# Splitting the feed-forward down products into three rounded products

## The reference, cut to what matters

```python
h = jnp.square(jax.nn.relu(jnp.einsum('bsd,fd->bsf', x, W_fc)))   # 256 -> 1024
y = jnp.einsum('bsf,df->bsd', h, W_proj)                          # 1024 -> 256
def step(mem, _):                                                 # five times
    reset = spike_fn(mem - THRESHOLD)
    mem_new = BETA * mem + y - reset * THRESHOLD
    return (mem_new, spike_fn(mem_new - THRESHOLD))
x = x + jnp.tanh(g_ffn[0]) * jnp.sum(spks, axis=0) / NUM_STEPS    # x: layernorm before W_fc
```

## Time and profile before

| | us |
|---|---|
| median of 3 runs (961.02 to 965.24) | 961.07 |
| profiled execution, its own time | 971.35 |
| its span | 969.6 |
| TensorE busy in it | 865.0 (89%) |
| VectorE, Pool, ScalarE busy | 546.8, 320.6, 306.4 |
| first up product to last down product of the feed-forward | 445.54 to 554.93 |

### The profile page before, as it was taken

One profiled execution on the slowest core, in us unless ns is written; L12 is line 12 of the kernel. 1 busy time (PEld: TensorE's weight loads), 2 busy tenths in 40 slices (PEclk: granted clock), 3 DMA queues, 4 the chain that ended last, 5 costly groups with the idle time before them and its releaser, 6 DMA issues.

```text
span 969.6 us, 12914 instructions
## 1 busy us (share of the span) xinstructions
PE 865.0 (89%) x4206; PEld 638.3 (66%) x4207; DVE 546.8 (56%) x1090; ACT 306.4 (32%) x656; POOL 320.6 (33%) x337
## 2 busy tenths in 40 slices
PE   6886699999785899987999979999999689999995
PEld 5454455554454555545888757777777579999994
DVE  4957646562476556642544378889888623333331
ACT  3555133233262333334333223222222012222230
POOL 4255244234146533441000114444443222232221
PEclk9999578899696889996999989999999879999999
DMA  9370000000000000008200082000000155555520
GB/s 302 117 308 27 1 0 1 1 1 1 0 1 0 1 1 0 1 1 288 55 0 0 1 283 75 11 12 11 12 11 12 54 192 198 201 167 168 200 81 4
DMA packets 32134, 67.87 MB, mean 70 GB/s; under 512 B 3161, under 2 KB 23095, under 8 KB 30999
## 3 DMA queue, kind: packets, MB, share of 16 engines
q1 hardware_dynamic: 28887, 56.63, 17.0%
q0 software_dynamic: 2624, 10.49, 3.4%
q10 hardware_dynamic: 578, 0.18, 0.1%
HBM read 55.20 MB, written 13.01 MB: 70 GB/s over the span
## 4 chain that ended last, share of the span: by engine, by line
PE 73%; DVE 15%; ACT 5%; issue 3%; DMA 2%; POOL 1%; DVEq 0%; SPq 0%; ACTq 0%; POOLq 0%
PE PS L1772 8%; PE PS L1760 8%; PE PS L639 7%; PE PS L1163 6%; PE PS L1145 6%; PE PS L1012 6%; PE PS L1000 5%; PE PS L630 4%; PE PS L610 4%; DVE NM L709 3%; PE PS L631 3%; PE PS L663 2%; PE PS L575 2%; PE PS L1147 2%; PE PS L649 2%
## 5 line engine op out<-in xcount | busy, mean ns | idle before, releaser
L817 ACT ACTIVATE EX<-PS 128x512 f32<-128x512 f32 x144 | 79.3, 594 | 173.2 <-PE PS L631 170.7
L709 DVE TENSOR_REDUCE NM<-PS 128x1 fp32r<-128x1101 f32 x64 | 82.7, 1302 | 73.9 <-PE PS L610 73.8
L800 POOL TENSOR_TENSOR sumP<-sumP,EX 128x1024 f32<-128x1024 f32 x32 | 75.8, 2368 | 42.2 <-ACT EX L817 41.2
L1760 PEld LDWEIGHTS PS<-xeT,w 128*128 128x128 f32 x736 | 85.7, 192 | 3.9 <-DMA w<-in_L_ffn_W 1.6
L1760 PE MATMUL PS<-xeT,w 128*128 128x128 f32 x736 | 86.1, 276 | 2.3 <-DMA w<-in_L_ffn_W 1.4
L1772 PE MATMUL PS<-w,heT 128*128 x368 | 83.3, 380 | 1.7 <-DVE oe L1702 1.7
L639 PE MATMUL PS<-EX,V 128*64 128x512 f32 (+1 forms) x288 | 75.3, 641 | 0.0
L1772 PEld LDWEIGHTS PS<-w,heT 128*128 128x128 f32 x368 | 68.3, 191 | 10.3 <-issue 2.1
L1163 PE MATMUL PS<-vw,pcT 128*128 128x256 f32 (+1 forms) x320 | 73.1, 384 | 1.2 <-ACT pcT L1355 1.2
L630 PE MATMUL PS<-QA,KA 100*128 100x512 f32 x144 | 70.3, 488 | 1.2 <-ACT EX L817 1.2
L1163 PEld LDWEIGHTS PS<-vw,pcT 128*128 128x128 f32 (+1 forms) x320 | 59.7, 191 | 8.8 <-issue 1.3
(11 more groups left out here) (260 smaller groups left out, 1586.9 us busy)
## 6 DMA issues: line engine op xcount, KB each, us to landing
w<-in_L_ffn_W SPq DMA_DIRECT2D x31, 1024.0 KB, 5.4
vw_rows<-vwn SPq DMA_DIRECT2D x2, 1232.0 KB
kwH_rows<-kwH SPq DMA_DIRECT2D x1, 2464.0 KB
kwL_rows<-kwL SPq DMA_DIRECT2D x1, 2464.0 KB
kwH<-kwH_rows POOLq DMA_DIRECT2D x1, 2464.0 KB, 12.5
kwL<-kwL_rows POOLq DMA_DIRECT2D x1, 2464.0 KB, 17.7
vw<-vw_rows SPq DMA_DIRECT2D x2, 1152.0 KB, 15.1
XR<-in_x SPq DMA_DIRECT2D x4, 512.0 KB, 14.2
```

Of the source, the lines that this page charges most:

```text
L709: dve.tensor_reduce(NM[:, n % 2, t // GT, SHIFT + t % GT:SHIFT + t % GT + 1], PSf[:, 512 * at:512 * at + KEYS], AX.X, ALU.max, negate=True ...
L800: pool.tensor_tensor(sumP[:], before, EX[:, (KT * n + c) % EB, :, :], ALU.add).then_inc(pool_summed, 1)
L817: act.activation(EX[0:r, k % EB, i, :], PS[0:r, ST_AT + i, :], ACT.Exp).then_inc(exp_done, 1)
L1760: last = pe.matmul(PS[:, 1 + 2 * p + c // 4, c % 4 * P:c % 4 * P + P], w1[:, u, k, c * P:c * P + P], xeT[:, p, k, :], start=k == 0, stop=k ...
```

## The change

The down products become three rounded products, as the up products are already. The inner values `h` get a high part `hH` (ScalarE's square, rounded on writing) and a rest `hL`: Pool computes the square once more in full format into one of two `square` tiles, and VectorE subtracts `hH` from it. The down weights get two parts in `wp`, made by Pool during the attention; the split of the up weights moves ahead of the first batch's attention, since `wp` takes the place of the unsplit up weights `wfc`. Two semaphores are new: `squared` (Pool's square is done) and `h_low` (VectorE's subtraction is done).

```diff
     def pe_ffn ... group
             pe.wait_ge(h_ready, FC * g + FC)
+            pe.wait_ge(h_low, FC * g + FC)
...
                     for c in range(FC):
-                        last = pe.matmul(PS[:, 4 + half, s * D:s * D + D], hT[:, c, at:at + P], wprojT[:, c, :],
-                                         start=c == 0, stop=c == FC - 1)
+                        for h, a in ((hH, 0), (hH, 1), (hL, 0)):
+                            last = pe.matmul(PS[:, 4 + half, s * D:s * D + D], h[:, c, at:at + P], wp[:, c, a, :],
+                                             start=c == 0 and h is hH and a == 0, stop=c == FC - 1 and h is hL)
...
     def act_ffn ... group
                 act.wait_ge(h_done, FC * g + c + 1)
+                if c >= 2:
+                    act.wait_ge(squared, FC * g + c - 1)
                 act.activation(relu[:, c % 2, :], PS[:, 2 + c % 2, :], ACT.Relu).then_inc(relu_ready, 1)
...
-                act.activation(hT[:, c, :], relu[:, c % 2, :], ACT.Square).then_inc(h_ready, 1)
+                act.activation(hH[:, c, :], relu[:, c % 2, :], ACT.Square).then_inc(h_ready, 1)
...
+    def pool_ffn(pool):
+        def group(g, last_group):
+            for c in range(FC):
+                pool.wait_ge(relu_ready, FC * g + c + 1)
+                if c >= 2:
+                    pool.wait_ge(h_low, FC * g + c - 1)
+                pool.tensor_tensor(square[:, c % 2, :], relu[:, c % 2, :], relu[:, c % 2, :], ALU.mult).then_inc(squared, 1)
+                if c == 1 and not last_group:
+                    pool_root(pool, g + 1)
...
     def dve_ffn
+        def low_parts(g, cs):
+            for c in cs:
+                dve.wait_ge(squared, FC * g + c + 1)
+                dve.wait_ge(h_ready, FC * g + c + 1)
+                dve.tensor_tensor(hL[:, c, :], square[:, c % 2, :], hH[:, c, :].bitcast(F32), ALU.subtract).then_inc(h_low, 1)
         z_low(0)
         with dve.Fori(0, NG - 1) as g:
             dve.wait_ge(g_zT, g + 1)
-            ffn_norm(dve, g + 1)
+            ffn_stats(dve, g + 1)
+            low_parts(g, range(4))
+            ffn_z(dve, g + 1)
+            low_parts(g, range(4, FC))
             z_low(g + 1)
             spike(g)
+        low_parts(NG - 1, range(FC))
...
+    def pool_wproj(pool):
+        pool.wait_ge(wfc_split, 2)
+        pool.tensor_copy(wp[:, :, 0, :], wprojT[:]).then_inc(wfc_split, 1)
+        pool.wait_ge(wfc_split, 3)
+        pool.tensor_tensor(wp[:, :, 1, :], wprojT[:], wp[:, :, 0, :].bitcast(F32), ALU.subtract).then_inc(wfc_split, 1)
...
         pool_project(pool, 0)
+        pool_wfc(pool)
         pool_attend(pool, 0)
         pool_project(pool, 1)
-        pool_wfc(pool)
+        pool_wproj(pool)
         pool_attend(pool, 1)
```

## The result

The changed kernel took 983.78 us (median of four runs, 979.2 to 988.66), the kernel before 963.15 beside it (961.02 to 965.24): a ratio of 1.0215, 95% interval 1.0143 to 1.0287. Slower, as forecast (983.7). The close agreement is luck: the four runs lie in two pairs, near 979.5 and 988.3, with the median between them, and the terms of the sum come to +17.4 us in the stage that the change touches, not to the +22.6 forecast. The same kernel run again (e0) gave 1.0142 [1.0098, 1.0186].

A forecast was written before the change was run, and what follows sets the result against it. TensorE's products were taken to bound the feed-forward stage. Terms 15.0 + 4.9 + 4.0 - 6.6 + 5.3 = +22.6 raised the profiled 971.35 to 994; less the profiled run's 10.3 above the median, 983.7 us, range 967 to 997.

The forecast's parts named there:

- waits, groups 1 to 4: Before each group's down products, the new square and subtraction chain adds 4.9, 7.5, 7.5 and 4.0 us.
- products: Down products on TensorE: 96 rounded products per group replace 64 records, 1.65 us less per group, -6.6 in all.
- clock: Down stages: TensorE's idle gaps make the granted clock fall in three of four, 1.75 us each, +5.3; bounds 0 and 7.
- Rival 1: Squares and subtractions run side by side without exclusion; only late root and longer chain count: +4.2, 965 us; chance 9%.
- I take 1.2: Pool's square of 512 columns takes 1.2 us, from a line through 462 and 1024 columns; bounds 0.60 and 1.3.
- I take 1.25: VectorE's four normalisations between the square and subtraction pairs cost 1.25 us, chosen between no cost and 1.38.
- The root's end: Pool's root in the middle groups ends at 483.6, 1.55 us after the statistics; squares three to eight wait behind it.
- two subtractions, 1.2: Last group: after the spike step ends at 533.5, two subtractions take 1.2 us before the third square begins at 534.7.
- the early release: Pool and VectorE exclude each other but for the last 0.15 us, so a square holds about 1.06, a subtraction 0.54.
- Linear between them: Down product of 256 columns takes 0.1295 us, between rows of 208 columns (0.110) and 512 columns (0.2335).
- Rival 3: Down products reach 0.110 us each, gaining 14.1 in all and outweighing the waits: 958 us, faster; chance 5%.
- Its other condition: The faster-products rival decides only if the waits before the down products stay under 14.1 us.

The follow-up runs named there:

- e0: The changed kernel run again with nothing altered: 979.91 us, ratio 1.0142 to the kernel before.
- e4: Changed kernel without Pool's squares and VectorE's subtractions, the third product taking the high part again: 953.24 us, ratio 0.9880 to the kernel before.
- e1: Changed kernel with VectorE's subtraction taking its first operand from an unused PSUM bank, square left out of the rest: 968.77 us, ratio 1.0044 to the kernel before.
- e3: Changed kernel with the next group's statistics and root taken one group earlier, full result computed: 975.52 us, ratio 1.0117 to the kernel before.
- e9: Changed kernel with both the subtraction reading PSUM (square left out) and the root one group earlier: 965.16 us, ratio 1.0014 to the kernel before.
- e5: Changed kernel with squares, subtractions and waits kept, but one full-format down product per chunk, rests left out: 992.34 us, ratio 1.0249 to the kernel before.
- e7: Changed kernel with 24 constant transposes (36 in the last group) on TensorE before the wait for the subtractions: 975.70 us, ratio 1.0105 to the kernel before.
- e2: Changed kernel with subtraction and normalisations of groups two to four reading PSUM, square and tokens left out there: 969.82 us, ratio 1.0044 to the kernel before.
- e11: Changed kernel with square on VectorE, subtractions mostly on Pool, root and normalisation earlier, TensorE kept busy by transposes: 962.58 us, ratio 1.0002 to the kernel before.

## Why the prediction was right, and where its sizes were off

| term, us | predicted | measured | by |
|---|---|---|---|
| waits, groups 1 to 4 | +4.9, 7.5, 7.5, 4.0 = 23.9 | +4.0, 6.7, 6.6, 2.8 = 20.1 | up to down, before and after |
| products | -6.6 | -9.3 | down stages of e4 against before |
| clock | +5.3 | +6.6 | down stages of after against e4 |
| sum in the stage | +22.6 | +17.4 | 126.77 - 109.39 |

*Mechanism.* It is the one forecast: Pool and VectorE take turns, the root stands ahead of the third square, and the clock falls. e1 and e3 take the first two away by themselves (8.1 and 6.5 us), e9 shows that they add up, and e5 that they don't hang on the products. Rival 1 (no exclusion, 965) falls with the subtractions of up to 1518 ns and with e1.

*Waits, 3.8 too high.* Three steps were off. "I take 1.2" for Pool's square: it takes 1.04 alone, and the line through 462 and 1024 columns overstates it. That is 0.3 per pair; the pairs end at 487.73 and 490.82 on Pool, 3.09 apart where I had 3.36. And "I take 1.25" for the normalisation: the next pair ends at 494.71, 3.89 later, so it cost 0.80. Together that is 1.2 in each of the first three groups, less 0.1 for the signal to TensorE (0.28 from the last subtraction's end, where I had 0.15).

The root's end was nearly right, 9.20 us after the first up product in the second group where I had 9.05 (483.6 - 474.55), but by two errors: the spike step ended 0.4 earlier than I had it, and the root took 2.08 from the end of the statistics for my 1.55, as its operations (0.48 and 1.32, before 0.23 and 1.04) ran beside the two subtractions behind the statistics. In the last group three pairs give 0.6 (9.70 from the third square to the down products, where I had 10.25), and "two subtractions, 1.2" another 0.7: the third square needs only the first of them and began at 547.54, 6.0 us after the first up product where I had 6.75.

The subtraction was right (0.68 for 0.69), and so was the early release: the spike step's last operation, beside a square that ended at 481.23, ended at 481.78. So 0.55 of its 0.75 lay behind the square, and it was let in 0.20 before the square's recorded end. By the Trainium skill ("SBUF — State Buffer", Who interferes with whom) whoever starts first keeps the shared ports for the whole instruction. The runs agree that the two take turns, but not to the recorded end: whole instructions of 1.04 and 0.68 would make two squares and two subtractions 3.44, against the 3.09 above.

*Products, 2.7 too little.* The step "Linear between them" gave 0.1295; e4 measures 0.120, midway to the 208-column row's 0.110. Over 384 products that is 3.7 us more gain; 1.0 of it went again, since the 14.08 that I removed holds the tail of the last products, and the first three down stages before last 13.73 up to the next up product. Rival 3's pace (0.110) was not reached. Its other condition failed too: waits of 20 us, not under 14.1. But without the new chain e4 shows a faster kernel, 0.988.

*Clock, 1.3 too little.* Four falls came, not three, each costing some 1.65 (6.6 / 4), close to the 1.75 read from the earlier trace rows. e7 ties the fall to TensorE's idle time: keeping it busy removes it without touching the wait. What decides exactly when it falls stays open: it fell in one down stage of e1, whose waits are longer than those of e9, where it fell in all four. TensorE's idle time just ahead of the down products doesn't tell them apart either: 1.9 to 2.6 us in e1, 2.3 to 2.6 in e9.

*From stage to time.* The stage's +17.4 stands against +20.6 between the first medians and +14.4 (979.91 - 965.50) in e0. So 983.7 was hit because the median of the first four runs lay high, and with it the kernel before, at 963.15 with its fourth run, 2.1 above the 961.07 that I added to; from the measured stage it would have been 961.07 + 17.4 = 978.5, inside the range.

## What to carry to other kernels

When work is split to run on a second elementwise engine beside the first, ask where each reads: two streams from SBUF on Pool and VectorE took turns here, and taking one operand from PSUM instead gave back 8 us of waits (e1, which leaves the square out of the result). Products made faster on the bounding engine pay only if the operands arrive at the pace of the faster products; the wait it opens costs a second time when the clock falls in it. A step whose inputs are ready early (here the statistics, root and normalisation of the next group) belongs where both engines idle, not between the links of a new chain.

## What the runs showed of the hardware that I had not expected

A rounded product of 256 columns takes 0.120 us from start to start with its weight load, and 0.214 at the half clock.

VectorE's normalisation has only one tensor input in SBUF (the two others are one value per partition), and it is stretched beside Pool all the same, from 399 to 1125 ns. Reading PSUM instead (e2) it keeps to 534 to 536 ns beside such squares. So "one SBUF tile", which rival 1 named as what lets an operation pass, does not hold for it.

Pool's subtraction of two different tiles into the rounded format takes 1.26 us at least, its square of one tile into full format 1.03.

Executions differ ahead of the stage that the change touches. Over the 14 traces, from before and after to e11, the feed-forward starts between 434.35 and 445.54 us, and the time that the granted clock spent at half ahead of it ranges from 105 to 128 us. The two go together (correlation 0.96; 0.44 us per us of half clock). So two executions can differ by some 10 us ahead of the stage without any change to it, the five medians of the kernel before taken beside these runs lie between 962.52 and 966.69, and the length of the touched stage tells more than one total.
